# Another order of the sixteen loads of the last stage of a fused graph kernel

## What is computed

```python
def _L0(x, evals, evecs, t):                     # evecs is adj
    x_spec = jnp.einsum('nk,nc->kc', evecs, x)
    coefs = jnp.exp(-evals * jnp.clip(t[0], 1e-08, None))[:, None]
    return jnp.einsum('nk,kc->nc', evecs, coefs * x_spec)

def _L1(inputs, adj, W, b):
    adj_hat = adj + jnp.eye(N)
    adj_norm = adj_hat / jnp.sum(adj_hat, axis=1, keepdims=True)
    return jnp.tanh(adj_norm @ (inputs @ W) + b)

x = _layernorm(x + _L0(x, evals, adj, t))
x = _layernorm(x + _L1(x, adj, W, b))
```

## Time and profile before

| | us |
|---|---|
| median of 3 executions | 619.7 (618.19 to 620.03) |
| the profiled execution, its own time | 618.76 |
| its span | 616.8 |
| TensorE busy in the span | 584.1 (95%) |
| VectorE | 509.7 (83%) |
| ScalarE | 398.4 (65%) |
| GpSimd | 366.6 (59%) |

### The profile page before, as it was taken

The page is one execution under the profiler, slowest core; times in us unless marked ns, Lnnn a source line. Parts: engine busy times, 40 slices in busy tenths (PEclk is TensorE's granted clock), DMA queues, the critical chain, the costliest instruction groups (busy, mean ns, idle before and its releaser), DMA issues.

```text
span 616.8 us, 8026 instructions
## 1 busy us (share of the span) xinstructions
PE 584.1 (95%) x2478; PEld 448.7 (73%) x2478; DVE 509.7 (83%) x572; ACT 398.4 (65%) x856; POOL 366.6 (59%) x215
## 2 busy tenths in 40 slices
PE   5999999999998989999999999999999869989993
PEld 5888888888876566768888788888888646746561
DVE  4899999999899988888899897795875748999992
ACT  4999999999996646365665545554454344445552
POOL 0000000000157887888999999778885697787882
PEclk9999999999999999999999999999999999999997
DMA  8999999999999999899959997489963899999101
GB/s 303 409 409 408 408 408 409 409 410 409 408 297 338 324 328 342 210 279 265 284 170 276 247 327 216 121 226 217 267 185 110 232 346 253 347 268 348 46 19 51
DMA packets 125066, 174.67 MB, mean 283 GB/s; under 512 B 6885, under 2 KB 105701, under 8 KB 125033
## 3 DMA queue, kind: packets, MB, share of 16 engines
q1 hardware_dynamic: 72608, 121.68, 59.8%
q10 hardware_dynamic: 52424, 52.58, 31.1%
HBM read 172.13 MB, written 2.11 MB: 282 GB/s over the span
## 4 chain that ended last, share of the span: by engine, by line
PE 79%; DVE 8%; POOL 6%; ACT 2%; ACTq 2%; issue 2%; DMA 1%; DVEq 0%
PE ps L835 14%; PE ps L837 13%; PE ps L836 13%; PE ps L807 9%; PE ps L809 9%; PE ps L808 9%; PE ps L831 7%; POOL lo L455 5%; DVE vt L664 3%; ACTq L353 2%; DVE lo L647 1%; PE ps L898 1%; PE ps L901 1%; PE ps L792 1%; POOL rstd L447 1%
## 5 line engine op out<-in xcount | busy, mean ns | idle before, releaser
L455 POOL TENSOR_TENSOR lo<-vt,hi 128x1024 fp32r<-128x1024 f32 x126 | 317.1, 2541 | 46.8 <-ACT hi L510 46.2
L664 DVE STREAM_TRANSPOSE vt<-raw 128x1024 f32<-128x1024 f32 x184 | 221.8, 1225 | 68.7 <-PE ps L837 58.2
L510 ACT ACTIVATE hi<-vt 128x1024 fp32r<-128x1024 f32 x159 | 165.1, 1060 | 105.9 <-DVE vt L664 87.9
L647 DVE TENSOR_TENSOR lo<-raw,hi 128x1024 fp32r<-128x1024 f32 x124 | 157.6, 1276 | 16.9 <-ACT hi L496 8.7
L496 ACT ACTIVATE hi<-raw 128x512 fp32r<-128x512 f32 x256 | 158.8, 623 | 5.5 <-DMA raw<-in_adj_dram 1.6
L421 POOL TENSOR_TENSOR lo<-raw,hi 128x1024 fp32r<-128x1024 f32 x4 | 10.2, 2561 | 169.7 <-ACT hi L496 169.7
L807 PE MATMUL ps<-hi,xg_hi 128*128 128x512 f32 x256 | 100.2, 391 | 1.5 <-DVE lo L647 1.4
L809 PE MATMUL ps<-hi,xg_lo 128*128 128x512 f32 x256 | 99.6, 389 | 0.0
L808 PE MATMUL ps<-lo,xg_hi 128*128 128x512 f32 x256 | 99.6, 389 | 0.0
L835 PE MATMUL ps<-hi,p_hi 128*128 128x512 f32 x206 | 88.4, 429 | 10.3 <-POOL lo L455 10.3
L835 PE MATMUL ps<-hi,s_hi 128*128 128x512 f32 x224 | 95.1, 425 | 3.1 <-POOL lo L455 2.6
(11 more groups left out here) (71 smaller groups left out, 535.4 us busy)
## 6 DMA issues: line engine op xcount, KB each, us to landing
raw<-in_adj_dram SPq DMA_DIRECT2D x63, 1024.0 KB, 15.8
raw<-in_adj_dram SPq DMA_DIRECT2D x90, 512.0 KB, 10.3
raw<-in_adj_dram ACTq DMA_DIRECT2D x88, 512.0 KB, 12.3
late_raw<-in_adj_dram SPq DMA_DIRECT2D x8, 512.0 KB, 11.9
late_raw<-in_adj_dram ACTq DMA_DIRECT2D x8, 512.0 KB, 14.1
xn<-in_x_dram SPq DMA_DIRECT2D x8, 256.0 KB, 15.4
x_sb<-in_x_dram SPq DMA_DIRECT2D x8, 256.0 KB, 13.7
out_dram<-x_sb ACTq DMA_DIRECT2D x7, 256.0 KB, 2.8
```

Source lines behind the costliest of these rows:

```text
L455: nc.gpsimd.tensor_tensor(lo[:, slot(p), :], vt[:, slot(p), :], hi[:, slot(p), :].bitcast(f32), ALU.subtract).then_inc(pool_lo_ready, 1)
L510: nc.scalar.activation(hi[:, slot(s), :], vt[:, slot(s), :], ACT.Copy).then_inc(hi_ready, 1)
L647: nc.vector.tensor_tensor(lo[:, q % RING1, :], raw[:, k, 2 * h:2 * h + 2, :].rearrange("p r n -> p (r n)"), hi[:, q % RING1, :].bitcast(f3 ...
L664: nc.vector.transpose(vt[:, slot(s), :].rearrange("p (m a i) -> p m a i", m=2, a=RB), load_buffer(st.load).rearrange("p (a m e i) -> p e m ...
```

## The change

```diff
-    ORDER3 = [(0, 0), (0, 1), (0, 2), (2, 1), (0, 3), (1, 1), (1, 2), (1, 3), (6, 3), (2, 2), (2, 3), (3, 2), (5, 3),
-              (3, 3), (4, 2), (4, 3)]
+
+    ORDER3 = [(0, 2), (0, 0), (2, 2), (0, 1), (0, 3), (2, 1), (2, 3), (1, 2), (1, 1), (1, 3), (6, 3), (3, 2), (3, 3),
+              (5, 3), (4, 2), (4, 3)]
```

## The result

| | before | after |
|---|---|---|
| median of 20 executions each, us | 619.06 (615.43 to 620.05) | 620.53 (618.27 to 622.13) |
| the profiled execution, its own time | 618.76 | 621.34 |
| its span | 616.8 | 619.4 |
| mean granted clock | 0.991 | 0.991 |

The ratio is 1.0032, with a 95% interval of 1.002 to 1.0044: 0.32% slower, about 2.0 us (1.2 to 2.7). Forecast were +2.2 us and 621.9; the range, 619.2 to 624.0, holds the time.

What follows compares the result with a forecast made beforehand. Stage 3 was taken as TensorE's work plus stretches where GpSimd's subtraction sets the pace. +2.35 - 0.15, with 0 from the start and VectorE's moves cancelling, gave +2.2 us: 620.9 profiled, 621.9 median, range 619.2 to 624.0.

Steps and rivals of the forecast that it cites:

- Steps 168 to 171: Two added GpSimd subtractions (169, 171) make GpSimd run without a break to step 174, which starts 2.35 us later.
- The start and the two D terms together: Steps 134-137 cost 0, and VectorE's two moved subtractions (147 to 149, 160 to 164) cancel: 0 in sum.
- After 174: Waits before 178 and 182 go, one group of output transposes comes in: about 0.15 us given back.
- Steps 134 to 137: Two removed subtractions lie ahead of GpSimd's idle time behind ScalarE's 6.29 us of issues; step 138 stays at 494.2: 0.
- the stated limit, 138 before 493: Sign that the prediction is wrong: TensorE starts step 138 before 493 us, where 494.2 was forecast.
- D from 147 to 149: VectorE's subtraction moved to 149: step 149 served, step 152 up to 0.8 us late, cost 0 to 0.3 us.
- D from 160 to 164: VectorE's subtraction moved to 164: second row's statistics up to 1 us earlier, step 166 up to 0.8 us earlier.
- Hidden: Rival: gains come in full, backlog at 171 under 1.8 us; +0.5 to +1.8 us; shares 0.31 with two other rivals.
- Faster: Rival: GpSimd has 171 ready when TensorE leaves 170, so TensorE sets the pace; -2.2 us, 617.5; chance 0.11.
- The start pays: Rival: `hi` of 138 comes 2.4 us earlier and cancels the late loss, 619.6; shares 0.31 with two other rivals.
- The clock falls: Rival: waits at 169 to 172 cause a second clock fall costing 1.7 us, 623.6; chance 0.06.
- the rival in which the first fall is avoided: Rival: the shorter wait before 138 undoes the clock fall at 505, returning 1.7 us, 620.2; shares 0.31 with two others.

Runs made afterwards that it cites:

- e2: Kernel before with steps 169 and 171 split as well, load order and VectorE's steps unchanged; 620.95 us, 1.0033 against before.
- e1: Changed kernel with steps 135 and 137 split again, VectorE's subtractions staying at 136, 149, 164, 180; 620.71 us, 1.0048 against before.
- e3: Changed kernel with VectorE's subtractions at steps 147 and 160 again instead of 149 and 164; 620.6 us, 1.0028 against before.
- e6: Changed kernel with ScalarE's four issues for the two late buffers moved four positions later, from 137 to 141; 622.72 us, 1.0067 against before.
- e10: Changed kernel with SyncE issuing all eight quarters of the two late buffers and ScalarE none; 619.58 us, 1.0021 against before.
- e4: Changed kernel with the subtraction of step 169 given to VectorE as well; 619.78 us, 1.0019 against before.
- e8: Changed kernel with the subtraction of step 171 given to VectorE as well; 620.14 us, 1.0023 against before.
- e7: Kernel before with the subtractions of steps 139 and 141 given to VectorE beside its own four; 618.37 us, 0.9988 against before.
- e9: Kernel before with SyncE issuing all eight quarters of the two late buffers and ScalarE none; 620.78 us, 1.0031 against before.

## Why the prediction was right, point by point

**Steps 168 to 171, +2.35: right.** `hi` 169 at 551.33 (forecast 550.93), `lo` 169 at 552.47 (552.0), no break to `lo` 174, step 174 at 565.94 (565.6). e2 shows by itself a loss of this size. The measured +2.49 from 134 to 174 and +1.56 from 166 to 174 differ because step 166 is itself 0.93 later; the forecast rested on `hi` 169 and not on step 166, and that was the right thing to rest it on. From `hi` 169 to step 174 lie 14.61 to 14.63 us in all five traces with the four split steps and the earlier third row (after, e1, e3, e6, e10), and the prediction's own times give 14.67. Only the waits before 170 to 172 were put too high, at 0.9 to 1.0 where 0.36 to 0.70 came. The prediction itself had the 0.7 from steps 139 to 141 and should have kept to it.

**The start and the two D terms together, 0: right in the sum, with luck in it.** At `hi` 169 they come to 0.17 us. On the way there the stretches moved by -0.85, +2.03 and -0.25, and neither the first nor the second was foreseen. The forecast of 621.9 for the median lies 1.4 above the 620.53 measured: the median before came out at 619.06 and not 619.7, and the difference at 2.0 by the ratio (1.5 by the medians) and not 2.2.

**After 174, -0.15: right.** -0.12; no wait before 178 and 182. From 184 the kernels run alike.

**Steps 134 to 137, 0: right in the sum, off in place.** Step 138 came 0.62 earlier (493.57, with a wait of 1.59, not 2.4), because the four issues took 5.45 us, not 6.29. The step that failed is "that block stands in front of step 138 in both kernels": it does, but not at one length. In the four traces whose steps 134 to 137 are as in the kernel after, with the issues in their place, it took 5.45 to 5.95 us (after, e3, e4, e8); in those that split all four it took 6.26 to 6.30 (before, e1, e2, e7). e1 has the new order of loads and still 6.26, so it goes with those steps and not with the order of the transfers; by what way stays open. The gain was gone by 152, and the stated limit, 138 before 493, wasn't reached.

**D from 147 to 149, 0 to 0.3: too low where it fell, right at the end.** VectorE's `lo` 149 took 3.42 us beside GpSimd, not 2.6, and step 149, said to be served, waited 0.58 for it (in e1 it took 1.18, with no wait); step 152 was 1.41 us later than before, not up to 0.8. Here the timeline of VectorE after:

```profile
516.17 3.42 DVE L672 TENSOR_TENSOR lo<-vt,hi 128x1024 fp32r<-128x1024 f32 x1
...
542.18 2.08 DVE L672 TENSOR_TENSOR lo<-vt,hi 128x1024 fp32r<-128x1024 f32 x1
```

**D from 160 to 164, a gain of 0 to 0.8: not seen.** The second line is `lo` 164, 2.08 us and so not alone; step 166 was 1.16 us later, not earlier. `lo` 162, said to start at 539.9 again, started at 540.82, since `lo` 160 started only at 536.80. I had also left out a small thing: two matmuls, 0.86 us together, that add group 1's saved sum stand ahead of 164 now and ahead of 156 before. At step 174 little of all this is left, by e1 and e3.

**The rivals.** *Hidden* asked that no more than 1.8 us reach step 174; 2.49 did in the profile. (The time alone, 1.2 to 2.7 us slower, doesn't rule it out.) *Faster* asked for GpSimd to have 171 ready; TensorE waited 0.67 for it. *The start pays* fell by e1, and for the stretch from 134 to 142 by e9 and e10, where a free ScalarE turned the removed subtractions into 0.05 us; what e10 gained behind that stretch stays open, as said above. *The clock falls*: no second fall; the granted clock is 1.00 from 545.3 to 563.2, through the waits of 0.4 to 0.7. The first fall stayed, at 0.65, though the waits ahead of it shrank from 3.14 to 1.59 at 138. Nor do such waits decide it alone. TensorE's timeline of e4, steps 138 and 142, and its windows view of 504 to 512 us:

```profile
494.37 0.50 PE L836 MATMUL ps<-hi,p_hi 128*128 128x512 f32 x1 [2.09 <-POOL lo L456]
...
505.38 0.49 PE L836 MATMUL ps<-hi,p_hi 128*128 128x512 f32 x1 [2.31 <-POOL lo L456]
...
504.00:512.00 8.00, 6.62 (x30) 4.79 (x31) 4.09 (x4) 4.41 (x9) 8.00 (x4) 1.00 1.10 347
```

Waits of that size, and the clock stays at 1.00 (2.4 GHz). Up to step 169 e4 and e8 are the same program as the kernel after. e8 waits 1.65 us before 138 and 2.30 before 142, the kernel after 1.59 and 2.30, and from 504 to 512 e8 has 1.00 where the kernel after has 0.79. So the same program has the fall of 1.7 us in some executions and not in others, which goes into the spread of a kernel's times (615.4 to 620.1 for before).

Whether the change makes the fall rarer isn't settled. The mean granted clock of an execution is 0.992 in the 20 of the kernel after, and 0.990 in the 96 of the kernel before that were timed beside the experiments. As an estimate from these two, 0.002 of a span of 617 us is 1.2 us. It could be why the average loss (2.0) is smaller than that of the profiled pair (2.6), in which each kernel has one fall, and then the rival in which the first fall is avoided is true in a part of the executions. But the means also hold the low clock at the end of the span, so none of this is shown.

## What to carry to other kernels

Count the operations that a reordering puts on the helping engine between two of its fixed points (here from `hi` 169, which stands behind a row's ending, to the next row's small operations): an engine busy 59% of the span set the time for 13 us, and two of its operations more there cost 2 us, while the two taken away from in front of a wait for another engine brought nothing. Before giving work to the engine that waits, ask what blocks the engine that it waits for; here it was ScalarE issuing transfers, and moving two of its four issues to SyncE (with one subtraction to VectorE) gave 0.9%. Moving all of them, or moving them later, gave nothing or a loss, because the wait turned up elsewhere.

## What was unexpected of the hardware

- Issuing a transfer can hold the issuing engine for microseconds, and more so with more transfers ahead of it. Four issues of 512 KB each took ScalarE 6.29 us at 484 us and 12.01 us at 492 us; two took 1.29. Six took SyncE 11.24 us, eight 22.40.
- Who issues a load changes when it lands. With all eight quarters from SyncE, VectorE waited for the second late load until 526.01; with six from SyncE and two from ScalarE it turned the first step of that load at 515.09 without a wait for a DMA.
- When the two engines' subtractions meet, one waits for the other, as the rows read. VectorE's, 1.18 us alone, took 2.08, 2.95 and 3.42 us beside GpSimd's and ended 1.08 to 1.09 us after it each time. Where VectorE's kept its 1.18, GpSimd's took 3.50 (e1) and not 2.4. Two starts 0.05 us apart went either way. So a subtraction given to VectorE doesn't always relieve GpSimd of the whole 2.35 us: in e8 its next one, `lo` 172, took 3.41.
